# A transformer block's projection written out in another order: early halves of batch 0's queries and keys, head 0's maxima spread over the later work

## The chip, the cores and the metric

One core of a Trainium2 chip runs the whole kernel. The metric is the device time of one execution in microseconds (us), as the median of several runs. The core has five engines with queues of their own: TensorE (PE, with its weight loads PEld), VectorE (DVE), ScalarE (ACT), GpSimd (POOL) and SyncE (SP), which here only issues transfers (DMAs). Engines wait for each other through semaphores, and each works its own queue strictly in order.

## The reference, cut to what matters

```python
h = layernorm(x) * (1 + ca) + sa                 # x: 2 x 2048 x 256, float32
Q, K, V = (lora_linear(h, W, b, A, B) for q, k, v)   # W x + b + 2 (x A^T) B^T, each 256 wide
energy = einsum('nqhd,nkhd->nhqk', Q, K) / sqrt(16)  # 16 heads of 16, batch of 2
out = einsum('nhqk,nkhd->nqhd', softmax(energy), V)
x = x + ga * lora_linear(out, Wo, bo, Ao, Bo)
h = layernorm(x) * (1 + cb) + sb
x = x + gb * (swiglu_shared(h) + swiglu_expert[argmax(h gate^T)](score * h))
```

sa, ca, ga, sb, cb, gb come from silu(c) times a 256 x 1536 matrix (`wmod`). The attention is 32 pairs of batch and head over 2048 positions. The change touches only the stage that makes Q, K and V and what runs beside it.

## The kernel before, in words

The 4096 rows of x are worked in eight chunks g of 512 rows (`NCH`); chunks 0 to 3 (`CPB` = 4) are batch 0, chunks 4 to 7 batch 1.

**One chunk.** SyncE loads x into one of two buffers (line 527). VectorE takes the moments (428, 432), ScalarE the root of the variance (`root`, 422), VectorE normalizes (`normalize`, 438 and 441). TensorE turns the chunk into banks 0 and 1 (581), ScalarE modulates it into hT (635). Then come four units of 128 channels, o = 0 and 1 for the two halves of the queries, 2 and 3 for the keys (`qk`, 587; banks 2 and 3 in turn), and two halves of the values (`v`, 596, bank 7, taken by VectorE at 680).

**One unit.** Scores need more than bf16, so each query and key is kept as three bf16 parts. ScalarE writes the unit as float32 (643) and its first part (645): this is `take`. GpSimd makes the remainder (723), ScalarE casts it to the second part (`middle`, 650), GpSimd makes the third part (727). SyncE stores the three parts to DRAM, 384 KB (535). There are four buffers of parts; a take waits until the store of the unit four before it has landed.

**A head's stack.** For its scores a head needs its 16 channels of the parts in 128 partitions. `stack` (771 to 786) reads them back with 16 copies: eight for `q_high` and `k_high`, whose sources have two parts (or the same part twice) as their leading dimension, and eight for `q_low` and `k_low`, each 16 rows. All 16 count on one semaphore, s_stack.

**Maxima.** The softmax needs the maximum of each row of energies first. `max_pair` (847) makes two 128 x 512 tiles of energies in a ring of three banks, VectorE reduces them (937). A head has 32 pairs. Later the negated maxima are turned, split by GpSimd and written by SyncE as two more rows of `q_low` (798), so that the scores (870) come out with the maximum taken off; `exps` (962) and the product with the values (881) follow. In the attention, head n's scores run beside the maxima of heads n+1 and n+2.

**The order before.** Every engine runs the chunks in order. Chunks 0 to 3 are a loop, 4 to 7 are written out. After the stores of chunks 0 to 3 have landed, SyncE issues head 0's stack, then the stores of chunk 4, the stack of head 1, small loads, the stores of chunk 5, the stack of head 2, three weight loads of 512 KB, and the other stores. Head 0's 32 pairs run beside chunks 4 to 7 (`BESIDE`: 2, 8, 11 and 11). Then come 12 pairs of head 1 with the matmuls of the modulation rows (915), and then head 0's scores.

Of the kernel before, what the change touches and what calls it, by code (L numbers as in the profile page):

```python
# [33 lines left out]
P = 128  # L34
# [29 lines left out]
STACK = 16 * 16  # L64
UQ = 2 * D // P
TAGS = 4
# [82 lines left out]
def block_kernel(nc, io, out):  # L149
    with ExitStack() as ctx:  # L150
# [81 lines left out]
        turned_sb = Region(nc, r.at, queries_at)("turned_sb", [KT, P])  # L232
# [74 lines left out]
        s_wT = sem("s_wT")  # L307
        s_wmod = sem("s_wmod")
# [137 lines left out]
        def setup_sync(sp):  # L446

            for dst, src in first_loads[:-1]:
                sp.dma_start(dst[:], src).then_inc(s_const, 16)
            sp.dma_start(wT[:], io["wT"]).then_inc(s_wT, 16)  # L450
            sp.dma_start(x_t[1][:], rows(io["x"], TPC, TPC)).then_inc(s_x[1], 16)
            dst, src = first_loads[-1]
# [3 lines left out]
            sp.dma_start(wmod[:, :, 512:], io["wmod"][:, :, 512:]).then_inc(s_wrow, 16)  # L456
# [10 lines left out]
        def setup_tensor(pe):  # L467
            pe.wait_ge(s_const, 16 * (len(first_loads) - 1))
            for m in range(4):
# [3 lines left out]
            mm.then_inc(s_lora, 1)  # L473
            pe.wait_ge(s_wmod, 16)
# [5 lines left out]
            mm.then_inc(s_mcol, 1)  # L480

        def setup_vector(dve, step):
            step(dve.memset(eps[:], EPS))
# [9 lines left out]
            dve.wait_ge(s_lora, 1)  # L493
            for m in range(4):
                dst = wqkv[:, m] if m < 3 else woT[:]
                w = dve.scalar_tensor_tensor(dst.rearrange("p k d -> p (k d)"), ps[:, 4 + m, :], LORA_SCALE,
                                             wT[:, m].rearrange("p k d -> p (k d)"), ALU.mult, ALU.add)
            w.then_inc(s_weff, 1)
# [4 lines left out]
            normalize(dve, step, 1, 1)  # L503
            dve.wait_ge(s_csilu, 1)
# [20 lines left out]
        def project_sync(sp):  # L525
            def load(g, u):
                sp.dma_start(x_t[u][:], rows(io["x"], g * TPC, TPC)).then_inc(s_x[u], 16)

            def store(g, b, j):

                for o in range(UQ):
                    half = o % 2
                    sp.wait_ge(s_qf_free, UQ + UQ * g + o + 1)
                    dst = qk_dram[o // 2].rearrange("s (b c) t -> c s b t", b=B)
                    sp.dma_start(dst[half * P:(half + 1) * P, :, bass.ds(b, 1), bass.ds(j * CH, CH)].squeeze(2),
                                 parts[o][:]).then_inc(s_parts[o], 16)

            with sp.Fori(0, CPB // 2) as i:
                for u in range(2):
                    g = 2 * i + u  # L540
                    sp.wait_ge(s_norm, g + 2)
                    load(g + 3, 1 - u)
                    store(g, 0, g)
            sp.wait_ge(s_norm, NCH - 2)
            load(NCH - 1, 1)
# [12 lines left out]
            for g in range(CPB + 2, NCH):  # L558
                store(g, 1, g % CPB)


        BESIDE = {CPB: 2, CPB + 1: 8, CPB + 2: 11, CPB + 3: PAIRS - 21}

        def units_beside(g):

            if g not in BESIDE:
                return iter(()), [0] * 7
            first = sum(n for c, n in BESIDE.items() if c < g)
            n = BESIDE[g]
            share = [0, 0, 0, 0, 0, 0, n] if g == CPB else [n * (i + 1) // 7 - n * i // 7 for i in range(7)]  # L570
            return iter(range(first, first + n)), share

        def project_tensor(pe):
            pe.sem_inc(s_v, 1)

            def turn(g, u):
                pe.wait_ge(s_norm, g + 1)
                wait(pe, s_hT, g)
                for k in range(HALF):
                    for t in range(TPC):  # L580
                        mm = pe.transpose(ps[:, k, t * P:(t + 1) * P], xn[u][:, t, k * P:(k + 1) * P], ident[:])
                mm.then_inc(s_xn_free, 1)

            def qk(g, u, o):
                pe.wait_ge(s_qbank_free, UQ * g + o + 1)
                for k in range(HALF):
                    mm = pe.matmul(ps[:, 2 + o % 2, :], wqkv[:, o // 2, k, (o % 2) * P:(o % 2 + 1) * P],  # L587
                                   hT[u][:, k, :], start=(k == 0), stop=(k == 1))
                mm.then_inc(s_unit, 1)

            def v(g, u, half):
                pe.wait_ge(s_vbank_free, 2 * g + half + 1)
                for c in range(2):
                    t = 2 * half + c
                    for k in range(HALF):
                        mm = pe.matmul(ps[:, 7, c * D:(c + 1) * D], hT[u][:, k, t * P:(t + 1) * P],  # L596
# [3 lines left out]
            def chunk(g, u):  # L600

                static = isinstance(g, int)
                units, share = units_beside(g if static else None)

                def beside(step):
                    for _ in range(share[step]):
                        max_pair(pe, (0, 0), next(units))

                if not static or g + 1 < NCH:
                    turn(g + 1, 1 - u)  # L610
                beside(0)
                pe.wait_ge(s_hT, g + 1)
                for step, (work, n) in enumerate(((qk, 0), (qk, 1), (v, 0), (qk, 2), (qk, 3), (v, 1))):
                    work(g, u, n)
                    beside(step + 1)

            turn(0, 0)
            pe.wait_ge(s_weff, 1)
            with pe.Fori(0, CPB // 2) as i:
                for u in range(2):  # L620
                    chunk(2 * i + u, u)
            for g in range(CPB, NCH):
                chunk(g, g % 2)

        def project_scalar(act):
# [5 lines left out]
            def modulate(g, u, b):  # L631
                act.wait_ge(s_xn_free, g + 1)
                wait(act, s_v, 1 + 2 * (g - 1))
                for k in range(HALF):
                    a = act.activation(hT[u][:, k, :], ps[:, k, :], ACT.Identity,
                                       bias=colmod[:, 0, k, bass.ds(b, 1)], scale=colmod[:, 1, k, bass.ds(b, 1)])
                a.then_inc(s_hT, 1)

            def take(g, o):
                bank, scale = 2 + o % 2, 0.25 if o < 2 else 1.0  # L640
                act.wait_ge(s_unit, UQ * g + o + 1)
                act.wait_ge(s_qf_free, UQ * g + o + 1)
                act.activation(qf[o][:], ps[:, bank, :], ACT.Identity, bias=bqk[:, o:o + 1], scale=scale)
                act.wait_ge(s_parts[o], 16 * (g + 1))
                act.activation(parts[o][:, 0, :], ps[:, bank, :], ACT.Identity, bias=bqk[:, o:o + 1],
                               scale=scale).then_inc(s_qbank_free, 1)

            def middle(g, o):
                act.wait_ge(s_rest, UQ * g + o + 1)
                act.copy(parts[o][:, 1, :], rest[o][:]).then_inc(s_mid, 1)  # L650

            def chunk(g, u, b, more, more2):

                if more:
                    modulate(g + 1, 1 - u, b)
                take(g, 0)
                take(g, 1)
                middle(g, 0)
                if more2:
                    root(act, g + 2)  # L660
                take(g, 2)
                middle(g, 1)
                take(g, 3)
                middle(g, 2)
                middle(g, 3)

            modulate(0, 0, 0)
            with act.Fori(0, CPB // 2) as i:
                for u in range(2):
                    chunk(2 * i + u, u, (2 * i + u + 1) // CPB, True, True)  # L670
            for g in range(CPB, NCH):
                chunk(g, g % 2, 1, g + 1 < NCH, g + 2 < NCH)

        def project_vector(dve, step):
            dve.sem_inc(s_vbank_free, 1)
            dve.wait_ge(s_bv, 16)

            def v(g, half):
                dve.wait_ge(s_v, 2 * g + half + 2)
                dve.tensor_tensor(v_all[:, bass.ds(TPC * g + 2 * half, 2), :],  # L680
# [3 lines left out]
            def chunk(g, u, nth, more2):  # L684
                units, share = units_beside(g if isinstance(g, int) else None)

                def beside(*steps):
                    for s in steps:
                        for _ in range(share[s]):
                            reduce_pair(dve, (0, 0), next(units))  # L690

                if more2:
                    moments(dve, step, g + 2, u, nth + 1)
                beside(0, 1, 2)
                v(g, 0)
                beside(3)
                if more2:
# [1128 lines left out]
```

## Time and profile before

| | |
|---|---|
| median of 3 runs | 1976.31 us (1973.0 to 1976.49) |
| profiled execution | 1975.94 us |
| its span | 1974.1 us |
| mean granted TensorE clock | 0.973 |
| PE busy | 1864.3 us (94%) |
| DVE busy | 1559.0 us (79%) |
| ACT busy | 1245.7 us (63%) |
| POOL busy | 341.5 us (17%) |
| maxima, L847 and L937 | 400.8 us of PE, 1273.3 us of DVE |

The profiled execution is 1.8 us longer than its span, which runs from the first to the last instruction. The shares are averages over the whole kernel. The projection and all that runs beside it fill the first 158 us; the attention lies behind it.

### The profile page before, as it was taken

What the parts mean: (1) busy time and instruction counts of PE and PEld (TensorE: products, weight loads), DVE (VectorE), ACT (ScalarE), POOL (GpSimd) and SP (SyncE); (2) the same over time, 40 slices, a digit from 0 to 9 for tenths busy, and PEclk for the clock granted to TensorE, in tenths of its full rate; (3) what the DMA queues carried; (4) which work ended last, traced back from release to release, by engine and by line L of the source; (5) the groups of instructions that cost most, each with busy time, mean ns of one, the idle gap of its engine ahead of it and who ended that gap; (6) DMA issues with size and microseconds to landing.
All of it is one profiled execution on the core that took longest, in us unless ns stands there. A gap on an engine that the chain in (4) does not pass through costs nothing.

```text
span 1974.1 us, 34939 instructions
## 1 busy us (share of the span) xinstructions
PE 1864.3 (94%) x13114; PEld 770.4 (39%) x13115; DVE 1559.0 (79%) x2738; ACT 1245.7 (63%) x1426; POOL 341.5 (17%) x425
## 2 busy tenths in 40 slices
PE   7687999999999999999999999999984799999997
PEld 5332222222222222222222222222224556589996
DVE  5376999999999999999999999999816732245553
ACT  4534777777777777777777777777871221144442
POOL 6534200000000000000000000000015622223332
PEclk9898999999999999999999999999997799999998
DMA  4541111211112111111112111111047432322221
GB/s 160 167 149 37 42 41 39 61 57 43 41 46 68 46 41 41 58 59 42 41 48 65 49 38 39 57 56 41 7 143 227 164 102 91 117 81 73 72 72 48
DMA packets 89737, 141.52 MB, mean 72 GB/s; under 512 B 13104, under 2 KB 60208, under 8 KB 89472
## 3 DMA queue, kind: packets, MB, share of 16 engines
q1 hardware_dynamic: 74336, 102.01, 16.5%
q0 software_dynamic: 10240, 32.40, 5.0%
q10 hardware_dynamic: 5024, 5.24, 0.8%
q8 instruction: 91, 1.49, 0.3%
q14 instruction: 46, 0.38, 0.1%
HBM read 90.84 MB, written 48.51 MB: 71 GB/s over the span
## 4 chain that ended last, share of the span: by engine, by line
PE 81%; DVE 9%; DMA 3%; POOL 2%; issue 2%; ACT 1%; SPq 1%; POOLq 0%; DVEq 0%; ACTq 0%
PE ps L881 24%; PE ps L870 20%; PE ps L847 15%; PE ps L1560 7%; DVE mx L937 6%; PE ps L1111 5%; PE ps L1583 3%; PE ps L1445 3%; DMA l_in<-inverse_sums 2%; PE ps L587 1%; ACT prob L962 1%; POOL parts L727 1%; POOL rest L723 1%; PE ps L915 1%; PE ps L596 1%
## 5 line engine op out<-in xcount | busy, mean ns | idle before, releaser
L937 DVE TENSOR_REDUCE mx<-ps 128x1 f32<-128x512 f32 x2048 | 1273.3, 683 | 58.7 <-PE ps L847 55.5
L962 ACT ACTIVATE prob<-ps 128x1024 f32<-128x1024 f32 x1024 | 992.4, 1021 | 275.1 <-PE ps L870 272.6
L881 PE MATMUL ps<-prob,vs 128*32 128x512 f32 x4096 | 546.5, 605 | 0.7 <-ACT prob L962 0.7
L847 PE MATMUL ps<-k_high,q_high 64*128 64x512 bf16 x2048 | 400.8, 388 | 33.3 <-DMA k_low<-qk_parts 16.8
L870 PE MATMUL ps<-q_high,k_high 64*128 64x512 bf16 x2048 | 389.8, 377 | 3.3 <-ACT prob L962 2.2
L870 PE MATMUL ps<-q_low,k_low 34*128 34x512 bf16 x2048 | 390.0, 377 | 0.0
L847 PEld LDWEIGHTS ps<-k_high,q_high 64*128 64x128 bf16 x2048 | 99.1, 93 | 668.4 <-DVE mx L937 628.1
L1016 POOL CAST mb<-turned_sb 16x128 bf16<-16x128 f32 x32 | 8.9, 279 | 925.3 <-ACT turned_sb L975 896.9
L870 PEld LDWEIGHTS ps<-q_low,k_low 34*128 34x128 bf16 x2048 | 100.0, 94 | 116.9 <-issue 0.5
L870 PEld LDWEIGHTS ps<-q_high,k_high 64*128 64x128 bf16 x2048 | 101.5, 96 | 88.7 <-ACT prob L962 30.0
L881 PEld LDWEIGHTS ps<-prob,vs 128*32 128x32 f32 x4096 | 80.7, 108 | 118.7 <-issue 113.4
L1646 DVE TENSOR_TENSOR ehT<-esig,ps 128x512 f32<-128x512 f32 x39 | 26.8, 688 | 100.6 <-PE ps L1560 100.6
L1466 ACT ACTIVATE sgate<-ps 128x512 f32<-128x512 f32 x32 | 19.1, 597 | 121.6 <-PE ps L1111 121.6
L1607 ACT ACTIVATE esig<-ps 128x512 f32<-128x512 f32 x39 | 23.3, 597 | 113.4 <-PE ps L1560 113.4
L1319 DVE TENSOR_TENSOR hid<-sgate,ps 128x512 f32<-128x512 f32 x32 | 22.0, 687 | 76.5 <-ACT sgate L1466 76.5
L1560 PE MATMUL ps<-xsT,gate_w 128*128 128x128 f32 x624 | 76.1, 275 | 1.6 <-issue 1.0
L1560 PEld LDWEIGHTS ps<-xsT,gate_w 128*128 128x128 f32 x624 | 75.6, 192 | 3.9 <-issue 1.2
L1560 PE MATMUL ps<-xsT,up_w 128*128 128x128 f32 x624 | 76.1, 275 | 0.0
L1583 PE MATMUL ps<-rdT,ehT 128*128 x312 | 73.6, 379 | 0.0
L1560 PEld LDWEIGHTS ps<-xsT,up_w 128*128 128x128 f32 x624 | 72.8, 192 | 0.0
L1136 PE MATMUL ps<-woT,o_in 128*128 128x256 f32 x128 | 38.5, 469 | 33.2 <-DVE o_in L1187 33.2
L1111 PE MATMUL ps<-h2T,wgT 128*128 (+1 forms) x128 | 64.0, 625 | 4.4 <-DVE x L1197 4.1
(146 smaller groups left out, 1416.4 us busy)
## 6 DMA issues: line engine op xcount, KB each, us to landing
k_high<-qk_parts SPq DMA_DIRECT2D x128, 128.0 KB
qk_parts<-parts SPq DMA_DIRECT2D x32, 384.0 KB, 3.8
q_high<-qk_parts SPq DMA_DIRECT2D x128, 64.0 KB
k_low<-qk_parts SPq DMA_DIRECT2D x128, 64.0 KB
head_out<-head_out_sb SPq DMA_DIRECT2D x32, 256.0 KB, 10.8
sorted_in<-zero_row POOLq DMA_DIRECT2D x13, 390.0 KB, 7.3
xs<-sorted_in SPq DMA_DIRECT2D x39, 130.0 KB
q_low<-qk_parts SPq DMA_DIRECT2D x128, 32.0 KB
```

What stands on the lines that cost most here:

```text
L847: pe.matmul(ps[:, ring.bank((n, m, u)), :], q_high[p][mine, t * P:(t + 1) * P], k_high[p][mine, c * CH:(c + 1) * CH], start=True, stop=Tru ...
L870: mm = pe.matmul(ps[:, 2 * i + u, :], keys[mine, kt * P:(kt + 1) * P], queries[mine, i * CH:(i + 1) * CH], start=(n == 0), stop=(n == 1))
L881: mm = pe.matmul(ps[32 * j:32 * j + 32, 7, :], vs[buf(h)][:, kt, :], prob[:, kt % 2, j * CH:(j + 1) * CH], start=(kt == 0), stop=(kt == KT ...
L937: dve.tensor_reduce(mx[n % 2][:, at, c:c + 1], ps[:, ring.bank(what), :], AX.X, ALU.max).then_inc(s_ring, 1)
L962: act.activation(prob[:, kt % 2, :].rearrange("p (u c n) -> p u c n", u=2, c=2)[:, :, half, :], ps[:, 2 * half:2 * half + 2, :], ACT.Exp). ...
L1111: mm = pe.matmul(ps[:, at, :], w[:, k, fc * P:(fc + 1) * P], h2T[:, k, bass.ds(g * CH, CH)], start=(k == 0), stop=(k == 1))
L1136: mm = pe.matmul(ps[:, OUT_BANK[u] + t // 2, t % 2 * D:(t % 2 + 1) * D], o_in[u][:, k, t * P:(t + 1) * P], woT[:, k, :], start=(k == 0), s ...
L1445: mm = pe.matmul(ps[:, DOWN_BANK[u] + t // 2, t % 2 * D:(t % 2 + 1) * D], hid[u][:, fc, t * P:(t + 1) * P], wdT[:, fc, :], start=(fc == 0) ...
L1560: mm = pe.matmul(ps[:, bank, fc * P:(fc + 1) * P], w[u][:, c, fc * P:(fc + 1) * P], xsT[u][:, c, :], start=(c == 0), stop=(c == 1))
L1583: mm = pe.matmul(ps[:, 6 + u, 0:D], ehT[u][:, c, :], rdT[:, bass.ds(e, 1), c, :].squeeze(1), start=(c == 0), stop=(c == FC - 1))
L1607: act.activation(esig[u][:].rearrange("p c n -> p (c n)"), ps[:, egate_bank(k), :], ACT.Silu).then_inc(s_esig, 1)
L1646: dve.tensor_tensor(ehT[u][:].rearrange("p c n -> p (c n)"), esig[u][:].rearrange("p c n -> p (c n)"), ps[:, eup_bank(k), :], ALU.mult).th ...
```

## The change

The loops become written-out code, and `BESIDE` goes away. A unit's number n = `unit(g, o)` now gives its place in the order, its bank (2 + n % 2) and its buffers (n % 4). hT has four buffers instead of two.

- **Early stage.** For chunks 0 to 3 only units o = 0 and 2 (first halves of queries and keys, heads 0 to 7) are made and stored: units 0 to 7. Head 0's stack is issued when these eight have landed.
- **Late stage.** The other units (8 to 15) and the values of chunks 0 to 3 follow; beside chunks 2 and 3 run 8 pairs of head 0, beside chunks 4 to 7 six each. Each pair stands behind one unit or one values half.
- **Setup.** The weights are loaded and adapted in two halves; wmod's later columns (1 MB) are loaded behind the stores of units 8 and 9 instead of at the start.
- **Roots.** ScalarE's root for chunk g+2 stands ahead of modulate(g+1) and the takes of chunk g in the early stage, and SyncE's load of chunk g+3 ahead of chunk g's two stores.
- **Stack.** The eight high copies are issued first and count alone on s_stack. The six low copies (the query lows merged to one copy for each half, 32 rows from parts 0 and 2) count on s_mrows, which the scores wait for.

```diff
-STACK = 16 * 16
+STACK = 16 * 8
+LOWS = 16 * 6
+MROWS = LOWS + 16 * 4
+EARLY = 2 * CPB
...
+        def unit(g, o):
+            return 2 * g + o // 2 if g < CPB and o % 2 == 0 else EARLY + 2 * g + o // 2 if g < CPB else UQ * g + o
...
 # project_sync
+            def load(g):
+                sp.wait_ge(s_norm, g - 1)
+                sp.dma_start(x_t[g % 2][:], rows(io["x"], g * TPC, TPC)).then_inc(s_x[g % 2], 16)
+            for g in range(CPB):
+                if g + 3 <= CPB + 1:
+                    load(g + 3)
+                store(g, 0, 2)
             for o in range(UQ):
-                sp.wait_ge(s_parts[o], 16 * (CPB + 1))
+                sp.wait_ge(s_parts[o], 16 * (EARLY // UQ + 1))
             stack(sp, (0, 0))
-            store(CPB, 1, 0)
+            load(CPB + 2)
+            store(0, 1, 3)
+            sp.dma_start(wmod[:, :, 512:], io["wmod"][:, :, 512:]).then_inc(s_wrow, 16)
+            store(1, 1, 3)
             stack(sp, (0, 1))
+            store(2, 1, 3)
+            load(CPB + 3)
             for dst, src in late_loads: ...
-            store(CPB + 1, 1, 1)
+            store(3, 1, 3)
             stack(sp, (0, 2))
             for dst, name in ((wgT, "wgT"), (wuT, "wuT"), (wdT, "wdT")): ...
-            for g in range(CPB + 2, NCH):
-                store(g, 1, g % CPB)
+            for g in range(CPB, NCH):
+                store(g, *range(UQ))
...
 # project_tensor
+            for g in range(CPB):
+                if g + 1 < CPB:
+                    turn_chunk(pe, g + 1)
+                pe.wait_ge(s_hT, g + 1)
+                qk(g, 0)
+                qk(g, 2)
+            pe.wait_ge(s_weff, 2)
+            for g in range(2):
+                qk(g, 1); v(g, 0); qk(g, 3); v(g, 1)
+            for g in range(2, CPB):
+                if g == CPB - 1:
+                    turn_chunk(pe, CPB)
+                for i in range(2):
+                    qk(g, 1 + 2 * i)
+                    max_pair(pe, (0, 0), 4 * (g - 2) + 2 * i)
+                    v(g, i)
+                    max_pair(pe, (0, 0), 4 * (g - 2) + 2 * i + 1)
+            for g in range(CPB, NCH):
+                if g + 1 < NCH:
+                    turn_chunk(pe, g + 1)
+                pe.wait_ge(s_hT, g + 1)
+                for i in range(2):
+                    first = 8 + 6 * (g - CPB) + 3 * i
+                    qk(g, 2 * i);     max_pair(pe, (0, 0), first)
+                    qk(g, 2 * i + 1); max_pair(pe, (0, 0), first + 1)
+                    v(g, i);          max_pair(pe, (0, 0), first + 2)
...
 # project_scalar: take(g, o) works on unit n
+                act.wait_ge(s_parts[slot], 16 * (n // UQ + 1))
+            for g in range(CPB):
+                root(act, g + 2)
+                if g + 1 < CPB:
+                    modulate(g + 1)
+                take(g, 0)
+                if g:
+                    middle(2 * g - 1)
+                take(g, 2)
+                middle(2 * g)
...
 # project_vector, from chunk 4 on
+                if g == CPB:
+                    moments(dve, step, CPB + 3, 1, (CPB + 3) // 2)
+                for i in range(2):
+                    reduce_pair x 2; v(g, i); reduce_pair
...
 # project_gpsimd
+            for first, end in ((0, EARLY), (EARLY, UQ * NCH)):
+                remainder(first)
+                for n in range(first + 1, end):
+                    remainder(n)
+                    last_part(n - 1)
+                last_part(end - 1)
...
 # stack
-                for n, (q_part, k_part) in enumerate(((2, 0), (0, 2))):
-                    sp.dma_start(q_low[p][at, :], q_parts[q_part, mine, cols]).then_inc(s_stack[p], 16)
-                    sp.dma_start(k_low[p][at, :], k_parts[k_part, mine, :]).then_inc(s_stack[p], 16)
+            for first, cols in halves:
+                sp.dma_start(q_low[p][first:first + LROWS, :], q_parts[0:3:2, mine, cols]).then_inc(s_mrows[p], 16)
+                for n, part in enumerate((2, 0)):
+                    sp.dma_start(k_low[p][at, :], k_parts[part, mine, :]).then_inc(s_mrows[p], 16)
```

## Rows read from the trace of the kernel before

**Rows 1.** Page, costliest groups: busy us, mean ns | idle before, releaser.
```profile
L847 PE MATMUL ps<-k_high,q_high 64*128 64x512 bf16 x2048 | 400.8, 388 | 33.3 <-DMA k_low<-qk_parts 16.8
```

**Rows 2.** Chain of waits, 66 to 100 us: start us, us, what.
```profile
72.50 3.92 DMA qk_parts<-parts
76.57 0.78 SPq L780
86.15 10.63 DMA k_low<-qk_parts
```

**Rows 3.** Windows: stretch, length, PE, PEld, DVE, ACT, POOL busy, granted clock, DMA, GB/s.
```profile
84.00:96.80 12.80, 0.00 (x0) 0.00 (x0) 0.00 (x0) 0.00 (x0) 0.00 (x0) 0.50 0.50 172
...
100.00:105.00 5.00, 5.00 (x13) 1.99 (x12) 3.24 (x12) 2.00 (x3) 0.00 (x0) 0.63 0.17 61
```

**Rows 4.** Timeline of PE: start us, us, instructions, count.
```profile
46.23 1.04 PE L581 MATMUL ps<-ident,xn 128*128 128x128 f32 x8
47.10 3.60 PE L587 MATMUL ps<-hT,wqkv 128*128 128x512 f32 x8
50.53 1.89 PE L596 MATMUL ps<-wqkv,hT 128*128 128x256 f32 x8
...
109.15 1.98 PE L587 MATMUL ps<-hT,wqkv 128*128 128x512 f32 x4
...
111.38 1.98 PE L587 MATMUL ps<-hT,wqkv 128*128 128x512 f32 x4
...
158.20 0.53 PE L847 MATMUL ps<-k_high,q_high 64*128 64x512 bf16 x2 [0.90 <-DVE mx L937]
...
180.71 0.38 PE L870 MATMUL ps<-q_high,k_high 64*128 64x512 bf16 x2
```

**Rows 5.** Timeline of ACT, in brackets the idle time before and its releaser.
```profile
26.63 0.69 ACT L643 ACTIVATE qf<-ps,bqk 128x512 f32<-128x512 f32 x1 [0.63 <-PE ps L587]
...
37.08 1.44 ACT L635 ACTIVATE hT<-ps,colmod 128x512 f32<-128x512 f32 x2
38.41 0.68 ACT L643 ACTIVATE qf<-ps,bqk 128x512 f32<-128x512 f32 x1
38.98 0.69 ACT L645 ACTIVATE parts<-ps,bqk 128x512 bf16<-128x512 f32 x1
...
40.94 0.62 ACT L650 CAST parts<-rest 128x512 bf16<-128x512 f32 x1
41.46 0.29 ACT L422 ACTIVATE std<-mv,eps 128x4 f32<-128x4 f32 x1
...
147.13 0.69 ACT L645 ACTIVATE parts<-ps,bqk 128x512 bf16<-128x512 f32 x1 [5.87 <-DMA qk_parts<-parts]
```

**Rows 6.** Timeline of POOL.
```profile
33.13 1.16 POOL L723 TENSOR_TENSOR rest<-qf,parts 128x512 f32<-128x512 f32 x1 [1.18 <-ACT parts L645]
```

**Rows 7.** Timeline of DVE.
```profile
35.97 1.39 DVE L428 BATCH_NORM_STATS2 stats<-x_t 128x6 f32<-128x256 f32 x4
37.51 0.38 DVE L432 BATCH_NORM_AGGREGATE mv<-stats 128x2 f32<-128x6 f32 x4 [0.15 <-DVE stats L428]
```

**Rows 8.** DMA view, 82 to 92 us, in 40 slices of 0.25 us.
```profile
GB/s 279 66 33 0 49 41 49 49 49 49 57 49 49 49 49 164 66 279 66 131 90 213 193 377 389 389 299 49 49 78 311 377 365 381 189 86 49 49 41 160
```

**Rows 9.** Copies: sizes from the page, landings of x loads, of stores from 86 us.
```profile
k_high<-qk_parts SPq DMA_DIRECT2D x128, 128.0 KB
...
q_high<-qk_parts SPq DMA_DIRECT2D x128, 64.0 KB
...
DMA to landing us min/median/max: 3.7/4.4/7.4
...
DMA to landing us min/median/max: 2.9/9.2/15.9
```

**Rows 10.** Timeline of SP: third stack's first copy, then stores of chunks 6, 7.
```profile
118.57 0.64 SPq L780 DMA_DIRECT2D q_high<-qk_parts  x1
...
131.24 26.05 SPq L535 DMA_DIRECT2D qk_parts<-parts  x8
```

More of the change, by code:

```diff
@@ L465, in setup_scalar, with adapt @@
             root(act, 1)
-        def setup_tensor(pe):
-            pe.wait_ge(s_const, 16 * (len(first_loads) - 1))
-            for m in range(4):
+        def unit(g, o):
+            return 2 * g + o // 2 if g < CPB and o % 2 == 0 else EARLY + 2 * g + o // 2 if g < CPB else UQ * g + o
+        def adapt(pe, first):
+            for m in range(first, first + 2):
                 for k in range(HALF):
@@ L473, in setup_tensor, with turn_chunk @@
             mm.then_inc(s_lora, 1)
+        def turn_chunk(pe, g):
+            pe.wait_ge(s_norm, g + 1)
+            wait(pe, s_hT, g)
+            for k in range(HALF):
+                for t in range(TPC):
+                    mm = pe.transpose(ps[:, k, t * P:(t + 1) * P], xn[g % 2][:, t, k * P:(k + 1) * P], ident[:])
+            mm.then_inc(s_xn_free, 1)
+        def setup_tensor(pe):
+            pe.wait_ge(s_const, 16 * (len(first_loads) - 1))
+            adapt(pe, 0)
             pe.wait_ge(s_wmod, 16)
@@ L480, in setup_tensor, with effective @@
             mm.then_inc(s_mcol, 1)
+            turn_chunk(pe, 0)
+            adapt(pe, 2)
         def setup_vector(dve, step):
+            def effective(first):
+                dve.wait_ge(s_lora, first // 2 + 1)
+                for m in range(first, first + 2):
+                    dst = wqkv[:, m] if m < 3 else woT[:]
+                    w = dve.scalar_tensor_tensor(dst.rearrange("p k d -> p (k d)"), ps[:, 4 + m, :], LORA_SCALE,
+                                                 wT[:, m].rearrange("p k d -> p (k d)"), ALU.mult, ALU.add)
+                w.then_inc(s_weff, 1)
             step(dve.memset(eps[:], EPS))
@@ L492, in setup_vector @@
             dve.wait_ge(s_wT, 16)
[L493 to L498, printed above, removed]
+            effective(0)
             dve.wait_ge(s_mcol, 1)
@@ L525, in project_sync, with store @@
         def project_sync(sp):
[L526 to L533, printed above, removed]
[L534 to L545 removed]
+            def load(g):
+                sp.wait_ge(s_norm, g - 1)
+                sp.dma_start(x_t[g % 2][:], rows(io["x"], g * TPC, TPC)).then_inc(s_x[g % 2], 16)
+            def store(g, *which):
+                for o in which:
+                    n, half = unit(g, o), o % 2
+                    sp.wait_ge(s_qf_free, UQ + n + 1)
+                    dst = qk_dram[o // 2].rearrange("s (b c) t -> c s b t", b=B)
+                    b, j = g // CPB, g % CPB
+                    sp.dma_start(dst[half * P:(half + 1) * P, :, b:b + 1, j * CH:(j + 1) * CH].squeeze(2),
+                                 parts[n % UQ][:]).then_inc(s_parts[n % UQ], 16)
+            for g in range(CPB):
+                if g + 3 <= CPB + 1:
+                    load(g + 3)
+                store(g, 0, 2)
             for o in range(UQ):
[L547 removed]
+                sp.wait_ge(s_parts[o], 16 * (EARLY // UQ + 1))
             sp.wait_ge(s_rows, 1)
             stack(sp, (0, 0))
[L550 removed]
+            load(CPB + 2)
+            store(0, 1, 3)
+            sp.dma_start(wmod[:, :, 512:], io["wmod"][:, :, 512:]).then_inc(s_wrow, 16)
+            store(1, 1, 3)
             stack(sp, (0, 1))
+            store(2, 1, 3)
+            load(CPB + 3)
             for dst, src in late_loads:
                 sp.dma_start(dst[:], src).then_inc(s_late, 16)
[L554 removed]
+            store(3, 1, 3)
             stack(sp, (0, 2))
@@ L557, in project_sync, with qk, v @@
                 sp.dma_start(dst[:], io[name]).then_inc(s_shared, 16)
-            for g in range(CPB + 2, NCH):
-                store(g, 1, g % CPB)
[L562 to L571, printed above, removed]
+            for g in range(CPB, NCH):
+                store(g, *range(UQ))
         def project_tensor(pe):
             pe.sem_inc(s_v, 1)
-            def turn(g, u):
-                pe.wait_ge(s_norm, g + 1)
-                wait(pe, s_hT, g)
+            def qk(g, o):
+                n = unit(g, o)
+                pe.wait_ge(s_qbank_free, n + 1)
                 for k in range(HALF):
[L580 to L588, printed above, removed]
+                    mm = pe.matmul(ps[:, 2 + n % 2, :], wqkv[:, o // 2, k, (o % 2) * P:(o % 2 + 1) * P],
+                                   hT[g % CPB][:, k, :], start=(k == 0), stop=(k == 1))
                 mm.then_inc(s_unit, 1)
-            def v(g, u, half):
+            def v(g, half):
                 pe.wait_ge(s_vbank_free, 2 * g + half + 1)
@@ L595, in v @@
                     for k in range(HALF):
-                        mm = pe.matmul(ps[:, 7, c * D:(c + 1) * D], hT[u][:, k, t * P:(t + 1) * P],
+                        mm = pe.matmul(ps[:, 7, c * D:(c + 1) * D], hT[g % CPB][:, k, t * P:(t + 1) * P],
                                        wqkv[:, 2, k, :], start=(k == 0), stop=(k == 1))
                 mm.then_inc(s_v, 1)
[L600 to L611, printed above, removed]
-                pe.wait_ge(s_hT, g + 1)
-                for step, (work, n) in enumerate(((qk, 0), (qk, 1), (v, 0), (qk, 2), (qk, 3), (v, 1))):
-                    work(g, u, n)
-                    beside(step + 1)
@@ L617, in project_tensor @@
[L617 to L621, printed above, removed]
-            for g in range(CPB, NCH):
-                chunk(g, g % 2)
+            pe.wait_ge(s_weff, 1)
+            for g in range(CPB):
+                if g + 1 < CPB:
+                    turn_chunk(pe, g + 1)
+                pe.wait_ge(s_hT, g + 1)
+                qk(g, 0)
+                qk(g, 2)
+            pe.wait_ge(s_weff, 2)
@@ L648, in middle @@
[L648 to L655, printed above, removed]
-                take(g, 0)
-                take(g, 1)
[L658 to L662, printed above, removed]
-                take(g, 3)
-                middle(g, 2)
-                middle(g, 3)
@@ L667, in project_scalar @@
[L667 to L670, printed above, removed]
-            for g in range(CPB, NCH):
-                chunk(g, g % 2, 1, g + 1 < NCH, g + 2 < NCH)
+                n = unit(g, o)
+                slot, bank, scale = n % UQ, 2 + n % 2, 0.25 if o < 2 else 1.0
+                act.wait_ge(s_unit, n + 1)
+                act.wait_ge(s_qf_free, n + 1)
+                act.activation(qf[slot][:], ps[:, bank, :], ACT.Identity, bias=bqk[:, o:o + 1], scale=scale)
@@ new lines, in project_scalar @@
+            middle(EARLY - 1)
+            for g in range(CPB):
+                if g == CPB - 1:
+                    modulate(CPB)
+                take(g, 1)
+                if g:
+                    middle(unit(g - 1, 3))
+                if g == CPB - 1:
+                    root(act, CPB + 2)
+                take(g, 3)
+                middle(unit(g, 1))
+            for g in range(CPB, NCH):
+                if g + 1 < NCH:
+                    modulate(g + 1)
+                for o in range(UQ):
+                    take(g, o)
+                    middle(unit(g, o) - 1)
+                    if g == CPB and o == 1:
+                        root(act, CPB + 3)
@@ L674, in project_vector @@
+            middle(UQ * NCH - 1)
         def project_vector(dve, step):
             dve.sem_inc(s_vbank_free, 1)
-            dve.wait_ge(s_bv, 16)
             def v(g, half):
                 dve.wait_ge(s_v, 2 * g + half + 2)
-                dve.tensor_tensor(v_all[:, bass.ds(TPC * g + 2 * half, 2), :],
+                dve.tensor_tensor(v_all[:, TPC * g + 2 * half:TPC * g + 2 * half + 2, :],
                                   ps[:, 7, :].rearrange("p (c d) -> p c d", d=D),
                                   bv_row[:].unsqueeze(1).to_broadcast([P, 2, D]), ALU.add).then_inc(s_vbank_free, 1)
[L684 to L694, printed above, removed]
+            for g in range(2, CPB + 2):
+                moments(dve, step, g, g % 2, g // 2)
+                normalize(dve, step, g, g % 2)
@@ L695, in chunk @@
+            dve.wait_ge(s_bv, 16)
+            for g in range(2):
                 v(g, 0)
-                beside(3)
-                if more2:
-                    normalize(dve, step, g + 2, u)
-                beside(4, 5)
                 v(g, 1)
-                beside(6)
-            with dve.Fori(0, CPB // 2) as i:
-                step.turns(i, 4)
-                for u in range(2):
-                    chunk(2 * i + u, u, i, True)
-            step.close(CPB // 2, 4)
-            for g in range(CPB, NCH):
-                chunk(g, g % 2, g // 2, g + 2 < NCH)
+            for g in range(2, CPB):
+                if g == CPB - 1:
+                    moments(dve, step, CPB + 2, 0, (CPB + 2) // 2)
+                for i in range(2):
+                    reduce_pair(dve, (0, 0), 4 * (g - 2) + 2 * i)
+                    v(g, i)
+                    reduce_pair(dve, (0, 0), 4 * (g - 2) + 2 * i + 1)
@@ new lines, in project_vector @@
+            normalize(dve, step, CPB + 2, 0)
+            for g in range(CPB, NCH):
+                if g == CPB:
+                    moments(dve, step, CPB + 3, 1, (CPB + 3) // 2)
+                for i in range(2):
+                    first = 8 + 6 * (g - CPB) + 3 * i
+                    reduce_pair(dve, (0, 0), first)
+                    reduce_pair(dve, (0, 0), first + 1)
+                    v(g, i)
+                    reduce_pair(dve, (0, 0), first + 2)
+                if g == CPB:
+                    normalize(dve, step, CPB + 3, 1)
```

75 lines of the change are left out of this document (41 added, 34 removed).

## The prediction

> **What bounds the kernel now.** I read the page first: of all matmul groups only the maxima's waits for a transfer at any length, 16.8 us of its 33.3 us idle, once [rows 1]. The chain of waits says where: the last store of the projection's first four chunks lands at 76.4 us, the first copy of head 0's stack is issued at 76.57, and the last lands at 86.15 + 10.63 = 96.8 us [rows 2]. The windows show TensorE without an instruction from 84 to 96.8 at a granted clock of 0.50, still 0.63 over 100 to 105 us (the 1.2 and 2.4 GHz levels mixed) [rows 3]. In TensorE's timeline batch 0's chunks follow each other without gaps; the first maxima of head 1 start at 158.20 and head 0's first scores at 180.71 [rows 4]. From there on nothing that the change touches sets the pace, so the forecast is one number: how far those scores move. The stretch 158.2 to 180.7 (twelve pairs of head 1, modulation rows) is unchanged, so I ask when the projection ends, against 158.2.
>
> **Durations.** At full clock one query or key unit takes (50.53-47.10)/2 = 1.72 us, a chunk's transposes 47.10-46.23 = 0.87. With a pair of maxima behind each unit (or values half, which is as long), the step is 111.38-109.15 = 2.23 us [rows 4]. ScalarE: modulate 38.41-37.08 = 1.33, a take twice 0.57 = 1.15, a middle cast 41.46-40.94 = 0.52, root 0.3 [rows 5]. GpSimd: 1.15 for a remainder or a last part [rows 6]. VectorE: moments 37.89-35.97 = 1.9 [rows 7]. An x load lands 4.4 us (median) after its issue, an unobstructed store 2.9 [rows 9].
>
> **The early stage.** The setup is reordered by a few us that nearly cancel: the first half of the weights is ready sooner, and modulate(1) stands behind root(2), which needs chunk 2's moments. I let the first take begin at 25.4 us, where it was 26.63 [rows 5]; it could be 2 us off either way. Ideally a chunk would cost only ScalarE's two takes, two casts, modulate and root, some 5.2 us. But root(g+2) now stands at the head of ScalarE's turn g, and SyncE issues the load of chunk g+2 behind the stores of chunk g-2, the second of which waits for a last part that GpSimd does only behind the remainder of take(g-1,0). So for chunks 4 and 5 there is a ring: two issues 0.8, load 4.5, moments 1.9, root 0.3, modulate 1.3, take 1.15, remainder 1.15, last part 1.15 = 12.3 us. The first two takes, a middle and root(3) end at 25.4+1.15+1.15+0.5+0.3 = 28.6 (a wait for the remainder included in the rounding), modulate and take(1,0) at 31.1 and, two GpSimd operations on, the last part of unit 1 at 33.4; that of unit 3 follows 12.3 later, 45.7. Root(5) is at 45.7+0.4+4.5+1.9+0.3 = 52.8, take(3,0) ends at 54.0, five GpSimd instructions bring unit 7 to 59.8, and its store lands at 63.5 (3.9 as in [rows 2]). ScalarE idles twice some 7 us. So the stack starts 13 us earlier than 76.57, where eight units rather than sixteen suggest twice that.
>
> **The stack.** It takes 20.2 us now from first issue to last landing, though its issues take 10. The transfer row shows why: in long stretches, with a dozen copies queued, 49 GB/s and no more move, while a store beside it runs at 300 to 390 [rows 8]. The eight high copies are 4 x (131+65.5) = 786 KB [rows 9], at 49 GB/s 16.0 us; with 2.2 us of latency (an unobstructed store's 2.9 less its own 1.0, rounded up) that leaves 2 us for everything else. So highs run on a narrow lane, and holding the lows back gains 1 to 2 us only: highs land at 63.5+2.2+16.0 = 81.7 us, 15 earlier than now.
> The Trainium skill ("DMA: Bandwidth & Descriptors", "Why a DMA increments its semaphore by 16 and not by 1") says that a copy is spread over the largest k up to 16 that divides the slowest dimension of both access patterns: 2 for the highs, whose source leads with two parts, 16 for the stores and for lows of 16 rows. The trace agrees (49 against 390 GB/s [rows 8]). By that rule the change's merged query lows, which also lead with two parts, go narrow; without it a stack would cost 2.4 us less.
> In rows: the new q_low copy has the shape of a q_high copy, 65.5 KB, two of them, 2.7 us at 49 GB/s, where before four of 32 KB cost the lane next to nothing. Bounds: 0 and 2.7 us a stack; I take 2.7, by the row of its own shape. A stack then fills the lane for 16.0+2.7+0.7 = 19.4 us.
>
> **What hangs behind the lane.** A store or load is spread wide, but ends only when the narrow engines have worked off what was queued before it: stores behind stacks land up to 15.9 us after issue instead of 2.9 [rows 9], and the last such store held ScalarE 5.87 us, until 147.13 [rows 5]. Its share of a narrow engine (24.5 GB/s) is 1.0 us a store, 1.3 a load of 512 KB, 2.7 for wmod's megabyte, which the change moves from 14.6 us into this queue. In before all of this gates only chunk 7. Now take n waits for the store of unit n-4, and three stacks stand before the store of unit 16, chunk 4's first. The lane, from 65.7: highs 81.7; lows 85.1; load 6 86.4; stores 8 and 9 88.4; wmod 91.1; store 10 92.1. Store 11 needs the last part behind take 12, which waits for store 8: 93.2. Second stack 112.6; store 12 113.6; store 13 and load 7 116; store 14 117. Store 15 needs the remainder behind take 16, which waits for store 12: issued 116.5, landed 119.4. Third stack 138.8; three weight loads 142.8; store 16 143.8. The same sum for the third stack of before (from 118.57 [rows 10], weights, store) gives 142.8 where 147.1 (131.2+15.9 [rows 9, 10]) is seen, since the lane was not empty at its start; I add 3 and put store 16 at 147.
> VectorE waits too: chunk 7's moments stand ahead of the maxima of chunk 4, and load 7 lands about 116, so TensorE stalls some 14 us at the second pair of chunk 4, with all that is queued behind it. That stall and the one at unit 18 are covered by the later one: unit 22, chunk 5's third, needs take 20, which needs store 16.
>
> **The sum.** TensorE would be at unit 22 about 138. Take 20 ends at 147.6. Behind it: half of chunk 5, 3 x 2.23 = 6.7; chunk 6, six steps and transposes, 14.4; chunk 7 13.4; together 34.5, so 182.1; the clock lost in a 10 us gap costs about 2.5 (the restart at 96.8 ran at half speed to about 103, which cost 3 [rows 3]): 184.5. That is 26 us after 158.2. I round to 25: the profiled run, 1975.94 us (span 1974.1), goes to 2001. The median, 1976.31, lies 0.4 off, which I leave out. Merging q_low also lengthens each later stack by 2 us in the attention; max pairs need only the highs, so this is hidden, at worst some us once. The split semaphores cost nothing: lows are due only at the scores, tens of us later. The written-out loops save at most a few tenths.
>
> **Rivals.**
> *Stores don't queue behind the stacks.* All else as above, TensorE sets the end: 82.0, then 0.3+6.7+1.0+9.0 for chunks 2 and 3, 3 x 14.4, 13.4 and 3 for the cold start = 158.6: no change, 1976. For it: TensorE is never idle in batch 0. Against: 15.9 us landings.
> *The early ring doesn't bind.* The stack starts 14 us earlier, everything behind by as much: +11, 1987. For it: now the loads never hold anything after 20 us. Against: their issue was not behind ScalarE's own wait.
> *Faster: eight highs back to back aren't held to 49 GB/s.* Issued in 8 x 0.65 = 5.2 us, they would land about 72, the later stacks would leave the lane in half the time, and TensorE alone would set the end: 72+76.6 = 148.6, 10 us early, 1966. It decides once store 16 lands before 158.2-35.1 = 123. For it: the two busier slices between the 49s. Against: their sum over a whole stack.
> *Both the first two at once*: 1963.
>
> **Chances.** Forecast 0.72 (own range 1989 to 2012), early ring free 0.08, stores free 0.08, highs fast 0.08, both free 0.04. Faster by over 0.2% (4 us, what a measurement here tells from none) 0.12, within 0.08, slower 0.80. The range takes in the case of no change: 1975 to 2014.
>
> **What would show it.** Right: ScalarE idle twice for 5 to 8 us before 54, waiting for chunk 4's and 5's moments; first maxima about 82; ScalarE waiting for stores at units 12, 16 and 20; VectorE waiting for x to about 116; TensorE idle up to about 147; scores at 206. Wrong: first maxima near 70, stores behind a stack landing within 5 us, or head 1's maxima starting before 158.

## The result and the profile after

The changed kernel takes 2000.9 us (median of 4 runs, 1998.5 to 2002.1) where the kernel before, run beside it, takes 1974.65: a ratio of 1.0132, 95% interval 1.0115 to 1.0150. Its profiled span is 2000.0 us, against 1974.1: 25.9 us more. The forecast was 2001.

The chain of waits of the changed kernel, 59 to 156 us (start us, us, what), shows where the time goes. It answers to [rows 2]:

```profile
59.71 3.60 DMA qk_parts<-parts
63.46 0.75 SPq L810
...
76.33 12.79 DMA qk_parts<-parts
89.14 0.70 ACT parts L671
89.91 1.15 POOL rest L757
91.06 1.12 POOL parts L762
92.60 0.64 SPq L810
...
105.28 11.58 DMA qk_parts<-parts
116.89 0.70 ACT parts L671
...
120.36 0.60 SPq L810
...
135.81 14.96 DMA qk_parts<-parts
150.80 0.70 ACT parts L671
151.54 3.78 PE ps L602 x4
```

Three times the same knot: SyncE issues a stack, then a store; the store lands 12 to 15 us later; the take that waited for it (units 12, 16, 20) runs; its remainder and last part release the next store and, twice, the next stack. ScalarE's timeline (in brackets the idle time before and its releaser) has the two waits of the early ring and these three, which answer to the one of 5.87 us in [rows 5]:

```profile
40.32 0.30 ACT L428 ACTIVATE std<-mv,eps 128x4 f32<-128x4 f32 x1 [7.03 <-DVE mv L438]
...
52.49 0.30 ACT L428 ACTIVATE std<-mv,eps 128x4 f32<-128x4 f32 x1 [7.20 <-DVE mv L438]
...
89.14 0.69 ACT L671 ACTIVATE parts<-ps,bqk 128x512 bf16<-128x512 f32 x1 [16.61 <-DMA qk_parts<-parts]
...
116.89 0.69 ACT L671 ACTIVATE parts<-ps,bqk 128x512 bf16<-128x512 f32 x1 [10.51 <-DMA qk_parts<-parts]
...
150.80 0.69 ACT L671 ACTIVATE parts<-ps,bqk 128x512 bf16<-128x512 f32 x1 [14.07 <-DMA qk_parts<-parts]
```

TensorE's timeline, which answers to [rows 4]: first maxima, the stall behind chunk 7's load, the stall behind unit 16's store, the first maxima of head 1 and the first scores:

```profile
83.53 0.61 PE L878 MATMUL ps<-k_high,q_high 64*128 64x512 bf16 x2 [11.72 <-DMA k_high<-qk_parts]
...
121.73 0.60 PE L878 MATMUL ps<-k_high,q_high 64*128 64x512 bf16 x2 [13.85 <-DVE mx L968]
...
151.54 3.78 PE L602 MATMUL ps<-hT,wqkv 128*128 128x512 f32 x4 [10.73 <-ACT parts L671]
...
189.83 0.39 PE L878 MATMUL ps<-k_high,q_high 64*128 64x512 bf16 x2 [1.15 <-DVE mx L968]
...
207.57 0.38 PE L901 MATMUL ps<-q_high,k_high 64*128 64x512 bf16 x2
```

Head 0's maxima do begin 13.3 us earlier (83.53 against 96.82), but head 0's scores begin 26.9 us later (207.57 against 180.71). From there to the end both kernels need the same time within 1 us (1792.4 and 1793.4).

### The profile page after: what moved, and what is told of

Same layout as the page of the kernel before. It is cut to its first block, busy times and chain, and to the rows that moved or that the text cites. A ratio compares the mean times of both kernels' runs of the same rounds, so it can differ in the third digit from the quotient of the medians.

```text
span 2000.0 us, 34634 instructions
## 1 busy us (share of the span) xinstructions
PE 1873.1 (94%) x13114; PEld 772.9 (39%) x13115; DVE 1557.8 (78%) x2738; ACT 1245.6 (62%) x1426; POOL 342.4 (17%) x425
## 4 chain that ended last, share of the span: by engine, by line
PE 80%; DVE 8%; DMA 5%; SPq 3%; ACT 2%; issue 1%; POOL 1%; POOLq 0%; DVEq 0%; ACTq 0%
PE ps L912 23%; PE ps L901 19%; PE ps L878 14%; PE ps L1591 7%; DVE mx L968 6%; PE ps L1142 5%; PE ps L1614 3%; PE ps L1476 3%; DMA qk_parts<-parts 2%; DMA l_in<-inverse_sums 2%; ACT prob L993 1%; PE ps L602 1%; SPq L817 1%; PE ps L1167 1%; PE ps L611 0%
## 5 line engine op out<-in xcount | busy, mean ns | idle before, releaser
L901 PEld LDWEIGHTS ps<-q_low,k_low 34*128 34x128 bf16 x2048 | 99.9, 94 | 116.9 <-issue 0.2
L1497 ACT ACTIVATE sgate<-ps 128x512 f32<-128x512 f32 x32 | 19.1, 597 | 121.8 <-PE ps L1142 121.8
L602 PE MATMUL ps<-hT,wqkv 128*128 128x512 f32 x128 | 69.0, 672 | 23.2 <-ACT parts L671 23.2
```

The source lines that it names most:

```text
L602: mm = pe.matmul(ps[:, 2 + n % 2, :], wqkv[:, o // 2, k, (o % 2) * P:(o % 2 + 1) * P], hT[g % CPB][:, k, :], start=(k == 0), stop=(k == 1))
L901: mm = pe.matmul(ps[:, 2 * i + u, :], keys[mine, kt * P:(kt + 1) * P], queries[mine, i * CH:(i + 1) * CH], start=(n == 0), stop=(n == 1))
```

## The experiments

Each is timed beside the kernel before on the same chip (1973.4 us in the first four, 1974.0 in the others). The changed kernel wasn't repeated there; at its ratio it stands for 1999.4 in the first four and 2000.1 in the others, and the gains below are told against these. The starts are read from one traced execution of each kernel.

**1. The early ring.** Loads of x ahead of the early stores.

```diff
-            for g in range(CPB):
-                if g + 3 <= CPB + 1:
-                    load(g + 3)
-                store(g, 0, 2)
+            for g in range(3, CPB + 2):
+                load(g)
+            for g in range(CPB):
+                store(g, 0, 2)
```

> Changed kernel with the x loads of chunks 3, 4 and 5 issued ahead of all early stores. My theory (a ring of store, load, moments, root holds ScalarE twice for 7 us, and everything behind it moves with the stack): both idle times of ScalarE before the roots vanish, unit 7's store lands at about 50 us instead of 63.5, head 0's scores start 13 us earlier, 1987 us. Rival (the early stage is paced by something else, or its gain is swallowed by the copies that queue later): scores within 3 us of 207.6, 2000 us.

Measured: 1989.4 us, ratio 1.0075 (1.0056 to 1.0094). Both waits before the roots are gone, and the stack starts at 52.78 us instead of 63.46. Scores start at 197.96, 9.6 us earlier. So the ring is real and moves all that follows, but it was worth 10 us, not the 13 expected: another wait took part of its place. ScalarE's timeline of this kernel:

```profile
33.43 0.34 ACT L428 ACTIVATE std<-mv,eps 128x4 f32<-128x4 f32 x1
33.63 1.48 ACT L660 ACTIVATE hT<-ps,colmod 128x512 f32<-128x512 f32 x2
34.95 0.73 ACT L669 ACTIVATE qf<-ps,bqk 128x512 f32<-128x512 f32 x1
37.53 0.69 ACT L671 ACTIVATE parts<-ps,bqk 128x512 bf16<-128x512 f32 x1 [1.84 <-DMA qk_parts<-parts]
...
42.04 0.69 ACT L669 ACTIVATE qf<-ps,bqk 128x512 f32<-128x512 f32 x1 [1.44 <-PE ps L602]
```

Unit 4's take now waits 1.84 us for unit 0's store, 1.44 us more are lost to TensorE behind it.

**2. The narrow copies.** Each high copy cut in two copies of 16 rows.

```diff
-                    at = slice(first + part * LROWS, first + (part + 1) * LROWS)
-                    sp.dma_start(q_high[p][at, :], q_parts[0:2, mine, cols])...
-                    sp.dma_start(k_high[p][at, :], k_parts[part:part + 1].to_broadcast([2, B * D, S])[:, mine, :])...
+                    for twin in range(2):
+                        at = slice(first + part * LROWS + twin * DH, first + part * LROWS + (twin + 1) * DH)
+                        sp.dma_start(q_high[p][at, :], q_parts[twin, mine, cols])...
+                        sp.dma_start(k_high[p][at, :], k_parts[part, mine, :])...
```

> Changed kernel with each high copy of a stack, whose source leads with two parts, cut into two copies of 16 rows (16 high copies instead of 8, the same bytes; the merged query lows are left as they are). My theory (the high copies move at 49 GB/s whatever else is free, and stores end behind them): highs land about 73 us instead of 83.5, stores behind a stack land within 6 us, the waits of ScalarE at units 12, 16 and 20 vanish, a stall of some 5 us for load 7 stays, scores start at 168 to 174 instead of 207.6, 1962 to 1968 us. Rival (the stack is limited by its issues and the latency of many copies): eight more copies make it 2 us longer, 2002 us. Rival (TensorE and the maxima set the end, not the stores): only the first 10 us count, 1990 us.

Measured: 1976.1 us, ratio 1.0017 (1.0007 to 1.0027); span 1972.3. With the same bytes in twice as many high copies the kernel gains 23 us, and its scores start at 181.94, 25.6 us earlier. The DMA view shows the rate while the first stack is under way: first the changed kernel, 66 to 84 us in slices of 0.45 us, then this one, 62 to 82 us in slices of 0.5 us.

```profile
GB/s 46 41 27 46 36 55 46 55 50 46 55 59 182 27 46 55 164 46 36 55 55 55 173 146 82 146 303 330 237 107 66 46 59 46 218 391 310 55 207 387
```
```profile
GB/s 6 0 0 0 66 131 115 111 127 94 119 82 131 70 135 66 131 66 131 0 127 164 33 123 168 90 152 127 174 289 377 385 383 154 88 100 143 229 297 346
```

About 50 GB/s become about 105. The windows say how many of the 16 DMA engines were at it: in the changed kernel, 66.3 to 71.0 us, their mean busy share is 0.12 at 46 GB/s, as if two of them worked; here, 64 to 70 us, it is 0.37 at 104 GB/s. SyncE issues a copy of 64 or 32 KB every 0.46 us, which makes 107 GB/s, so its issues alone can set the new rate (an estimate; no run tests it). The first maxima start at 72.14, as expected (73). But the waits didn't vanish, they shrank, as the first store behind each stack still lands after 5.6 to 9.1 us, and this is why the gain is less than the expected 35 us. ScalarE's and TensorE's timelines of this kernel:

```profile
81.93 0.69 ACT L671 ACTIVATE parts<-ps,bqk 128x512 bf16<-128x512 f32 x1 [9.95 <-DMA qk_parts<-parts]
...
102.99 0.69 ACT L671 ACTIVATE parts<-ps,bqk 128x512 bf16<-128x512 f32 x1 [7.82 <-DMA qk_parts<-parts]
...
127.81 0.69 ACT L671 ACTIVATE parts<-ps,bqk 128x512 bf16<-128x512 f32 x1 [5.07 <-DMA qk_parts<-parts]
```
```profile
107.68 0.61 PE L878 MATMUL ps<-k_high,q_high 64*128 64x512 bf16 x2 [11.00 <-DVE mx L968]
```

Chunk 7's load, which I had at 5 us of stall, still holds TensorE for 11: it is issued only at 98.31 us, behind the second stack and the last part that waits for unit 12's store.

**3. The merged query lows.** Four copies of 16 rows again instead of two of 32.

```diff
-                sp.dma_start(q_low[p][first:first + LROWS, :], q_parts[0:3:2, mine, cols])...
                 for n, part in enumerate((2, 0)):
                     at = slice(first + n * DH, first + (n + 1) * DH)
+                    sp.dma_start(q_low[p][at, :], q_parts[2 - part, mine, cols])...
```

> Changed kernel with each merged query low copy (two parts, 32 rows) issued as two copies of 16 rows again, four instead of two. My theory (the merged copies run at 49 GB/s and cost 2.4 us a stack): the store of unit 16 lands about 7 us earlier, at 144, 1994 us. Rival (two copies fewer are cheaper or the same): 2000 to 2001 us.

Measured: 1992.8 us, ratio 1.0100 (1.0085 to 1.0115). ScalarE's timeline:

```profile
143.46 0.69 ACT L671 ACTIVATE parts<-ps,bqk 128x512 bf16<-128x512 f32 x1 [10.55 <-DMA qk_parts<-parts]
```

The take behind unit 16's store runs at 143.46 instead of 150.80, 7.3 us earlier for three stacks: 2.4 us a stack, as worked out. That edit, meant to save a copy, is by itself 7 us of the 26.

**4. The last gate.** Head 2's stack behind the stores of chunk 6.

```diff
-            stack(sp, (0, 2))
...
             for g in range(CPB, NCH):
                 store(g, *range(UQ))
+                if g == NCH - 2:
+                    stack(sp, (0, 2))
```

> Changed kernel with head 2's stack issued behind the stores of chunk 6 instead of ahead of those of chunk 4. My theory (the last gate is unit 16's store behind that stack): ScalarE's wait at unit 20 (14 us) and TensorE's stall of 10.7 us vanish, with the restart at half clock, scores start 12 us earlier, 1988 us; the waits at units 12 and 16 stay. Rival (the gate behind it, TensorE with spread maxima, takes its place): 1996 to 2000 us.

Measured: 1992.5 us, ratio 1.0093 (1.0074 to 1.0111). The stall at unit 22 and the wait of 14 us are gone, and the maxima beside the modulation rows end at 193.96 us, 13.8 us earlier. But 4.8 us are given back at once, so that the scores start 8.8 us earlier and not the expected 12, as its chain of waits shows:

```profile
193.57 0.39 PE ps L879 x2
193.96 4.80 issue
198.76 1.05 PE ps L902 x4
```

SyncE's timeline names it: the stack now stands ahead of the last four stores. The rows of maxima that head 0's scores need are issued only when all stores have landed; SyncE waits 7.1 us for the last of them. GpSimd had these rows ready at 181.5, yet they go out at 194.91, 3.9 us ahead of the scores. In the changed kernel they go out at 195.33, as soon as they are ready, 12.2 us ahead of the scores.

```profile
180.46 7.22 SPq L568 DMA_DIRECT2D qk_parts<-parts  x4
194.91 2.72 SPq L830 DMA_DIRECT2D q_low<-mb  x4
```

**5. A stall said to be covered.** Chunk 7's load right behind chunk 6's.

```diff
             load(CPB + 2)
+            load(CPB + 3)
             store(0, 1, 3)
...
-            load(CPB + 3)
```

> Changed kernel with chunk 7's x load issued right behind chunk 6's, ahead of the second stack. My theory (the 13.9 us stall of TensorE at the second pair of chunk 4, which waits for this load through VectorE, is covered by the later wait for unit 16's store): the stall at 107.9 us shrinks to the wait for unit 12's store, TensorE instead waits longer at unit 22, scores start within 2 us of 207.6, 2000 us. Rival (each stall counts, they add up): 10 to 14 us earlier, 1986 to 1990 us.

Measured: 2004.3 us, ratio 1.0153 (1.0135 to 1.0171), so nothing gained; the interval overlaps that of the changed kernel. Scores start at 209.70, 2.1 us later. TensorE's timeline:

```profile
119.95 3.78 PE L602 MATMUL ps<-hT,wqkv 128*128 128x512 f32 x4 [7.21 <-ACT parts L671]
...
153.80 3.78 PE L602 MATMUL ps<-hT,wqkv 128*128 128x512 f32 x4 [17.13 <-ACT parts L671]
```

The stall of 13.85 us shrinks to one of 7.21, now at unit 18, and the one at unit 22 grows from 10.73 to 17.13: what one gives back the other takes. Here two stalls of TensorE don't add up, because the later gate, unit 16's store, didn't come earlier: it landed at 153.1 instead of 150.8.

**6. The same cure for the kernel before.** High copies of 16 rows, nothing else changed; the diff is that of experiment 2, with 24 copies on s_stack.

> Kernel before with each high copy cut into two copies of 16 rows, nothing else. My theory (the narrow high copies set the gap of 17 us before head 0's maxima): all 24 copies are issued in 11 us and land about 90 us instead of 96.8, ScalarE's wait of 5.87 us at 147 vanishes, scores start 6 to 8 us earlier, 1967 us against 1974. Rival (in the old order the stack is limited by issues and by the stores behind it): within 2 us of before, or later by the 4 us of added issues.

Measured: 1966.2 us, ratio 0.9965 (0.9952 to 0.9978). The first maxima start at 90.97 instead of 96.82, and no take waits for a store any more. Head 1's maxima start at 151.40, 6.8 us earlier. Scores start at 170.44 instead of 180.71, but 3.5 of these 10.3 us go with a higher granted clock in the stretch between (0.91 against 0.77), of which more below.

**7. Ring and narrow copies together** (experiments 1, 2 and 3 in one kernel).

> Changed kernel with the x loads of chunks 3 to 5 ahead of the early stores, and all copies of a stack cut to 16 rows (highs and query lows). My theory (the two causes are separate: the early ring costs 10 us as measured alone, the narrow copies 25): the gains add up, scores start at about 171, 1963 us, faster than before by 10; the stall for chunk 7's load stays at some 11 us. Rival (with the narrow copies gone the ring is hidden): 1972 us.

Measured: 1964.5 us, ratio 0.9957 (0.9943 to 0.9971). Scores at 169.57. The causes are separate to within 5 us: 2000.1 less 10, 23 and 7 would be 1960. The new order is now ahead of the old as it was, but its interval overlaps that of the old order with the same cure for its high copies (experiment 6), so these two can't be told apart.

**8. All four together**: 7 with the edits of 4 and 5.

> As the kernel with loads ahead and all copies of 16 rows, and besides chunk 7's x load behind chunk 6's and head 2's stack behind the stores of chunk 6. My theory (what is left are the stall for that load, 11 us, and the wait for unit 16's store, 2 to 5; then TensorE sets the end): scores start at 152 to 158, 1945 to 1952 us, the new order is faster than the old one by over 1%. Rival (the order itself, with 23 us more TensorE work behind the first maxima, can't beat the old one by more than the gap it closes): 1962 us or more.

Measured: 1957.4 us (median of 8, 1953.9 to 1974.5), ratio 0.9928 (0.9904 to 0.9951), the lowest median of all. Both the theory (1945 to 1952) and the rival (1962 or more) missed; scores start at 163.42, 5 us later than the range I gave. TensorE's timeline has two waits left that go back to stores (units 14 and 18); from 94.36 to 143 nothing interrupts it:

```profile
62.13 0.39 PE L879 MATMUL ps<-k_high,q_high 64*128 64x512 bf16 x2 [2.58 <-DMA k_high<-qk_parts]
...
74.73 1.98 PE L603 MATMUL ps<-hT,wqkv 128*128 128x512 f32 x4 [2.77 <-ACT parts L672]
...
94.36 1.98 PE L603 MATMUL ps<-hT,wqkv 128*128 128x512 f32 x4 [2.40 <-ACT parts L672]
...
144.28 0.39 PE L879 MATMUL ps<-k_high,q_high 64*128 64x512 bf16 x2 [1.15 <-DVE mx L969]
...
163.42 0.38 PE L902 MATMUL ps<-q_high,k_high 64*128 64x512 bf16 x2
```

Head 1's maxima start at 144.28, 13.9 us before the 158.20 of the old order, and with their modulation rows take 19.1 us more.

## Why the prediction was right, step by step

The sign, the size and the places are those of the forecast, and the experiments take its main terms away one by one. The last us are luck, as the sum below shows.

- *The early ring.* Waits of 7.03 and 7.20 us where "some 7" stood; unit 7's store landed at 63.3 (59.71 + 3.60), predicted 63.5. Shown by experiment 1; as a price I had 14 us for it, and it is 10.
- *Highs at 49 GB/s.* First maxima at 83.53, predicted 81.7. That the highs set this start is shown by experiments 2 and 6. Of the 1.8 us more, 0.6 go with the merged lows (82.92 in experiment 3); the rest is open.
- *Stores behind stacks.* The stores that takes 12, 16 and 20 waited for landed at 89.1, 116.9 and 150.8; I had 87.4, 113.6 and 147. By bytes alone the last would have been 143.8; the kernel before was 4.3 us above the same sum, of which I added 3 without saying why not the whole. Experiment 4 shows the third gate. That it is a few shared DMA engines, and not the queue as a whole, rests on the rates, on the busy share of 0.12 and on experiments 2 and 3; the views give the mean over the 16 engines and not what each of them carried.
- *Query lows.* 2.4 us a stack, shown by experiment 3.
- *VectorE behind chunk 7's load.* Waited until 119.18 (predicted about 116), TensorE 13.85 us (14). That it is covered is shown by experiment 5. VectorE's timeline:

```profile
119.18 1.40 DVE L434 BATCH_NORM_STATS2 stats<-x_t 128x6 f32<-128x256 f32 x4 [13.17 <-DMA x_t<-in_x]
```

- *The sum.* Two errors cancelled. Head 1's maxima began at 189.83, 5.3 us later than the 184.5 of my sum. Of this, 3.9 are take 20 (TensorE went on at 151.54 instead of 147.6) and 1.2 a wait for VectorE just before them, which the sum left out; the 37 us of work between came out right. And the stretch from there to the scores, which I carried over at 22.5 us, took 17.7. TensorE's first modulation matmuls of the kernel before, and the windows before (157 to 181 us) and after (188 to 208 us):

```profile
158.66 3.50 PE L915 MATMUL ps<-wmod,cB 128*128 128x512 f32 x4
```
```profile
157.00:181.00 24.00, 17.36 (x47) 5.32 (x48) 15.35 (x27) 2.59 (x5) 4.69 (x9) 0.79 0.11 35
```
```profile
188.00:208.00 20.00, 13.10 (x49) 4.30 (x49) 15.75 (x27) 3.22 (x6) 7.60 (x12) 1.00 0.21 66
```

VectorE has the same 15.4 to 15.8 us of work, but the granted clock is 1.00 instead of 0.79: of the levels 1.2 and 2.4 GHz, the kernel before falls to the lower one for part of the stretch. It had been granted 1.00 from 110 to 157 us, with TensorE busy 77% of the last 40 us, and fell as the stretch began. Why is open. The order alone doesn't decide it: experiment 6, with the old order and the same 77%, needs 19.0 us for the stretch, and experiment 8, with the new order and unbroken work ahead, 19.1, both at 0.91; the changed kernel and experiments 1, 2, 3, 5 and 7 need 17.7 at 1.00. So scores came 26.9 us later where the sum has 26.3, by luck in this part. The forecast of 2001 also rests on 26.3 being rounded to 25 without a reason; from the scores on, the changed kernel was 1.0 us shorter. The range, not the centre, is what the sum supports.

- *Rivals.* All fell. The fast one comes nearest: the highs as the change has them are held to 49 GB/s, but cut to 16 rows they aren't. That alone brings the new order within 0.2% of the old (1.0017); only with the ring and the lows mended too is it ahead (experiments 7 and 8).

## What to carry to other kernels

When a queue of transfers feeds a rotating set of buffers, write down for each transfer what stands ahead of it and which take waits for it: a transfer moved ahead of another costs nothing until the one behind it is waited for. Look at the rate between the bursts, not only at the mean over a stage: here a long plateau at an eighth of the peak, with 0.12 of the DMA engines busy, was made by copies whose outermost dimension is 2, and the stores issued behind them landed 12 to 15 us after issue. And starting a stage earlier pays only as far as the work left behind it doesn't grow: here seven more units, six more values halves and two more chunks of transposes stood behind head 0's first maxima, some 24 us of TensorE work at 1.72 and 0.87 us, and the gates were moved with it.

## What the runs showed of the hardware

- Cutting each high copy of 32 rows (leading dimension 2) into two of 16 rows raised the rate from about 50 to about 105 GB/s, and the busy share of the DMA engines from 0.12 to 0.37. The Trainium skill ("DMA: Bandwidth & Descriptors", "Why a DMA increments its semaphore by 16 and not by 1") says that a transfer uses the largest number of engines up to 16 that divides the slowest dimension of both access patterns, which is 2 for the one form and 16 for the other. The traces agree with it for the first form (0.12 of 16 is two), and experiments 2, 3 and 6 gain by the second.
- An issue on SyncE isn't of one length. In the changed kernel's first stack the low key copies took 2.29 and 2.38 us for two; the same copies took 0.41 or 0.42 each in the kernel before, and 0.42, with one of 0.76, in experiment 3. The whole stack of 14 copies took 12.4 us to issue (63.46 to 75.86), the 22 of experiment 2 only 10.6 (63.14 to 73.79). That the copies still under way hold the issuer back is a guess: the length of the queue isn't in the trace.
- The same twelve pairs and 16 modulation matmuls took 22.5 us at a granted clock of 0.77 (158.20 to 180.71 us of the kernel before), 19.0 and 19.1 at 0.91 (experiments 6 and 8) and 17.7 at 1.00. Neither the order of the kernel nor how busy TensorE was ahead of the stretch sorts these runs: it was busy 77% of the 40 us ahead in the kernel before and in experiment 6, and without a gap for the last 38 us in experiments 7 (17.7) and 8 (19.1). Why the clock falls or stays is open.
